# The four factors of the update of q in PSUM instead of SBUF

## The chip, the cores and the metric

One core of one Trainium2 chip runs the kernel. The metric is the device time of one execution in microseconds (us); lower is better. Engines are named as in the profile: PE is TensorE (PEld its weight loads), DVE is VectorE, ACT is ScalarE, POOL is GpSimd, SP is SyncE.

## The reference

The input x holds 16 sequences of 128 steps with 256 features. It drives an oscillator network, one Runge-Kutta step of fourth order per time step, and every q of it then goes through a feed-forward layer of eight experts (the best two taken) and a shared expert. The result is added to x.

```
def _derivative(q, p, drive, coupling, bias):
    i_couple = jnp.tanh(q) @ coupling.T
    dq = q - q ** 3 / 3.0 - p + drive + i_couple + bias
    dp = EPSILON * (q + ALPHA - BETA * p)
    return (dq, dp)

def _rk4_step(q, p, drive, coupling, bias):
    dq1, dp1 = _derivative(q, p, ...)
    dq2, dp2 = _derivative(q + 0.5 * DT * dq1, p + 0.5 * DT * dp1, ...)
    dq3, dp3 = _derivative(q + 0.5 * DT * dq2, p + 0.5 * DT * dp2, ...)
    dq4, dp4 = _derivative(q + DT * dq3, p + DT * dp3, ...)
    q_next = q + DT / 6.0 * (dq1 + 2 * dq2 + 2 * dq3 + dq4)
    ...
    q_next = jnp.clip(q_next, -CLAMP, CLAMP)
...
logits = x @ W_router.T            # x is here the trace of q
combine = top 2 of softmax(logits)
sh = silu(x @ gate) * (x @ up) @ Ws_down, times sigmoid(x @ W_sgate.T)
eo = the same for each of 8 experts, weighed with combine
x_out = x_in + shared + sparse
```

The 128 steps depend on each other, and so do the four derivatives in a step: 512 stages that can only run one after the other.

## The kernel before

Features lie on the partitions: 256 features are 2 halves (KC) of 128 partitions, with 16 sequences (B) each, so that every tile of the recurrence is 128x32. The program is written out in full: BLOCKS = 16 blocks of STEPS = 8 steps, with STAGES = 32 stages in a block. The order on each engine is the order in which the code emits it, and semaphores connect the engines.

A stage n goes as follows. PE (`couple`) first adds the drive into the bank `coup_ps` by three matmuls of an identity (line 554), behind which stand, in some stages, up to six matmuls that write columns 256 to 383 of that bank and whose result nobody reads (L558, counts in `WARM`). It then waits for ACT's first tanh, `th_hi` in fp16 (L439), and multiplies it with the two fp16 parts of the coupling (L565, eight matmuls). Then it waits for `th_lo` (L820, DVE), the rest of the tanh, which DVE takes from ACT's second tanh in PSUM (`th`, L440), and multiplies it (L571, four matmuls). The last of these counts up `summands`. DVE meanwhile works out the cubic term (L813 or ACT's L446, L817 or L824), the sums for p (L784), and `force` (L831), and then forms the next q:

```
dve.wait_ge(summands, 2 * (n + 1))
nc.vector.scalar_tensor_tensor(
    q_raw[:] if k == 3 else q_in[k + 1][:], coup_ps[:, 0:CB]...,
    c_un[:, ...], force[:], ALU.mult, ALU.add).then_inc(q_ready, 1)
```

This is line 848, once in each of the 512 stages. It multiplies the coupling with a factor and adds `force`. The factor is one value for each partition: a column of `c_un`, worked out on the chip before the first stage (L718: `unscale`, a power of two that depends on the coupling's largest element, times the step's constant C[k]). The instruction gets it as the address of a 128x1 operand, a pointer scalar. L784, L813, L817, L824 and L831 are the same kind of instruction (scalar_tensor_tensor) with their factor written in the instruction as a constant. `q_ready` releases ACT's tanh (L439), DVE's own square (L813) or clip (L794), and PE's next drive matmuls (L554).

Behind `couple` of each stage PE takes pieces of the feed-forward layer of the block before and of the one before that: router (L584), `comb` turned and spread (L592, L603), up projections (L629), down projections (L646). Tables such as `UP_AT` and `DOWN_AT` say in which stage. ACT and DVE have their parts of it (L480, L488; L895, and `route`, L859 to L873) between the recurrence's instructions.

Before the first stage DVE prepares the scales and constants one after the other; each `step` counts up `setup_v`. Step 10 is `ident_u` (L716), step 11 is `c_un` (L718), step 12 is `p_now` (L721).

Of the kernel before, what the change touches and what calls it, by code (L numbers as in the profile page):

```python
# [28 lines left out]
P = 128  # L29
# [130 lines left out]
def program(nc, x, cond, coupling, bias, w_up, w_down, w_route, identity, spread, iota, e_base, out):  # L160
    ctx = ExitStack()
    with ctx:
        def sb(name, shape, dt=F32):
            return ctx.enter_context(nc.sbuf_tensor(name, shape, dt))

        def pb(name):
            return ctx.enter_context(nc.psum_tensor(name, [P, 512], F32))

        def sem(name):
            return ctx.enter_context(nc.semaphore(name))  # L170
# [27 lines left out]
        ebits = sb("ebits", [P, 2], U32)  # L198
        scale = sb("scale", [P, 2])
        unscale = sb("unscale", [P, 2])  # L200
        c_un = sb("c_un", [P, 4])

        q_trace = sb("q_trace", [P, KC, STEPS, B])
        q_raw = sb("q_raw", [P, KC, B])
# [38 lines left out]
        coup_ps = pb("coup_ps")  # L243
# [4 lines left out]
        square_ps = pb("square_ps")  # L248
        th, square_first, square, cubic = [ps[:, c:c + CB].rearrange("p (m b) -> p m b", m=KC) for ps, c in (
            (th_ps, 0), (square_ps, 0), (square_ps, 2 * CB), (square_ps, 4 * CB))]  # L250
        comb_tp = route_ps[0:96, 64:128].bitcast(BF16)

        in_cf = sem("in_cf")
# [5 lines left out]
        setup_v = sem("setup_v")  # L259
# [100 lines left out]
        def upper(x, steps):  # L360

            return x[:, steps].rearrange("p t m b -> p (t m b)").bitcast(BF16)[:, 1::2]

        def flat(x, steps):

            return x[:, steps].rearrange("p t m b -> p (t m b)")
# [137 lines left out]
        def _(pe):  # L504
# [37 lines left out]
            def couple(b, st):  # L542

                n = b * STAGES + st
                if n == 0:
                    pe.wait_ge(setup_v, 10)
                else:
                    pe.wait_ge(q_ready, n)
                if st % (4 * HALF) == 0:
                    pe.wait_ge(x_split, 4 * b + 2 + 2 * (st // (4 * HALF)))  # L550
                t = b * STEPS + st // 4
                at = slice(t, t + 1)
                for x, piece in enumerate((upper(xb, at), upper(x_rest, at), flat(x_low, at))):
                    nc.tensor.matmul(coup_ps[:, 0:CB], ident_u[:], piece, start=x == 0, stop=False,  # L554
                                     skip_group_check=True)
                if n > STAGES:
                    for _ in range(WARM[st - 1]):
                        nc.tensor.matmul(coup_ps[:, 2 * P:3 * P], c16[:, 0, 0, 0:P], c16[:, 0, 0, 0:P],  # L558
                                         start=False, stop=True, skip_group_check=True)

                pe.wait_ge(hi_ready, n + 1)
                for part in range(2):
                    for m in range(KC):
                        for k in range(KC):
                            nc.tensor.matmul(coup_ps[:, m * B:(m + 1) * B], c16[:, part, k, m * P:(m + 1) * P],  # L565
                                             th_hi[:, k, :], start=False, stop=False, skip_group_check=True)

                pe.wait_ge(lo_ready, b * STAGES + st + 1)
                for m in range(KC):
                    for k in range(KC):  # L570
                        last = nc.tensor.matmul(coup_ps[:, m * B:(m + 1) * B], c16[:, 0, k, m * P:(m + 1) * P],  # L571
                                                th_lo[:, k, :], start=False, stop=True, skip_group_check=True)
                last.then_inc(summands, 1)
# [78 lines left out]
            def one_block(b):  # L652
                for st in range(STAGES):
                    couple(b, st)
                    prepare(b * STAGES + st)
                    if b == 1 and st == 0:
                        pe.wait_ge(in_wd, 2 * 16)
                        pe.wait_ge(in_const, 4 * 16)
                    for f, at in ffn_stages(b, st)[::-1]:
                        ffn(f, at)  # L660
                    if b == 0 and STAGES // 2 <= st < min(REST_AT):

                        for _ in range(8):
                            nc.tensor.matmul(up_ps[0][:, 0:P], c16[:, 0, 0, 0:P], c16[:, 0, 0, 0:P], start=True,
                                             stop=True)
# [358 lines left out]
```

## Time and profile before

| | |
|---|---|
| median of 3 runs | 655.67 us (655.66 to 658.51) |
| the profiled execution | 658.68 us |
| its span, first to last instruction | 656.9 us |
| granted TensorE clock, mean | 0.992 of full speed |
| busy share of the span | PE 97%, PEld 93%, DVE 93%, ACT 56%, POOL 30% |

Durations in the profile overlap where an engine is pipelined: an instruction on DVE can start while the records of the one ahead of it still run. So a busy share of 97% does not mean that the engine has no room. Distances from start to start, and from the end of one to the start of the one that waited for it, tell more.

### The profile page before, as it was taken

Reading aid. Unit: us, or ns where it says so; the run is one execution under the profiler, and the core shown is the slowest. Engines: PE = TensorE matmul, PEld = TensorE weight load, DVE = VectorE, ACT = ScalarE, POOL = GpSimd, SP = SyncE. Lnnn points to the kernel's source line nnn. Section 1 sums busy time; section 2 is a strip of 40 time slices with the busy share of each in tenths; the row PEclk is TensorE's granted clock in tenths of the full one; section 3 lists DMA queues with packets and bytes.
Section 4 is the critical chain, followed back from the end, with each engine's and each line's share of the span. In section 5 each row is a group of like instructions: output and inputs, shape, how many; then the busy total and the mean of one; then the engine's idle time right before and its main releaser. Section 6 shows DMA issues by size and latency. Waiting matters only on the chain.

```text
span 656.9 us, 33948 instructions
## 1 busy us (share of the span) xinstructions
PE 637.9 (97%) x12839; PEld 610.6 (93%) x12839; DVE 614.0 (93%) x4540; ACT 365.4 (56%) x1880; POOL 194.0 (30%) x436
## 2 busy tenths in 40 slices
PE   3899999999999999999999999999999999999998
PEld 2689899999999999999999999999999999999997
DVE  6998999999999999999999999999999999999951
ACT  4776655555555555556555555555556555554643
POOL 0002133242323334232333423233342323323244
PEclk9997999999999999999999999999999999999999
DMA  7800000000000000000000000000000000000000
GB/s 297 279 2 2 4 2 4 11 3 11 4 11 3 3 12 2 12 2 12 3 4 10 4 12 3 11 4 2 12 4 11 3 12 2 4 12 3 11 3 17
DMA packets 9059, 13.65 MB, mean 21 GB/s; under 512 B 1568, under 2 KB 8032, under 8 KB 8256
## 3 DMA queue, kind: packets, MB, share of 16 engines
q1 hardware_dynamic: 8896, 11.50, 5.2%
q8 instruction: 100, 1.64, 1.0%
q14 instruction: 63, 0.52, 0.3%
HBM read 9.40 MB, written 2.10 MB: 17 GB/s over the span
## 4 chain that ended last, share of the span: by engine, by line
PE 90%; DVE 8%; DMA 0%; issue 0%; ACT 0%; POOL 0%; DVEq 0%; SPq 0%
PE up_ps L629 28%; PE down_ps L646 21%; PE coup_ps L565 15%; PE coup_ps L571 13%; PE coup_ps L554 5%; PE coup_ps L558 3%; PE route_ps L603 2%; DVE q L848 1%; PE route_ps L584 1%; DVE w L772 1%; DVE force L831 1%; DVE th_lo L820 1%; DVE square_ps L817 1%; DVE square_ps L813 1%; DVE p_sum L784 1%; DVE y L784 0%
## 5 line engine op out<-in xcount | busy, mean ns | idle before, releaser
L629 PE MATMUL up_ps<-q_hi,w 128*128 128x128 f16 x2176 | 236.4, 219 | 0.2 <-POOL q_lo L926 0.2
L963 POOL TENSOR_TENSOR hidden<-hidden,comb_s 128x128 f32<-128x128 f32 x272 | 123.3, 456 | 297.7 <-ACT th_hi L439 290.2
L439 ACT ACTIVATE th_hi<-q 128x32 f16<-128x32 f32 x384 | 88.1, 229 | 213.6 <-DVE q L848 211.9
L629 PE MATMUL up_ps<-q_lo,w 128*128 128x128 f16 x1088 | 199.7, 220 | 0.0
L565 PE MATMUL coup_ps<-th_hi,c 128*128 128x16 f16 x4096 | 180.7, 171 | 0.2
L646 PE MATMUL down_ps<-hidden,wd 128*128 128x128 f32 x1088 | 180.8, 290 | 0.0
L629 PEld LDWEIGHTS up_ps<-q_hi,w 128*128 128x128 f16 x2176 | 176.2, 98 | 0.7 <-POOL q_lo L926 0.4
L565 PEld LDWEIGHTS coup_ps<-th_hi,c 128*128 128x128 f16 x4096 | 138.8, 96 | 4.6
L646 PEld LDWEIGHTS down_ps<-hidden,wd 128*128 128x128 f32 x1088 | 141.9, 191 | 0.0
L571 PE MATMUL coup_ps<-th_lo,c 128*128 128x16 f16 x2048 | 131.4, 173 | 0.4 <-DVE th_lo L820 0.3
L480 ACT ACTIVATE act_s<-up_ps,unscale 128x128 f32<-128x128 f32 x272 | 98.9, 364 | 13.8 <-PE up_ps L629 10.1
L629 PEld LDWEIGHTS up_ps<-q_lo,w 128*128 128x128 f16 x1088 | 105.9, 97 | 0.1
L554 PE MATMUL coup_ps<-xb,ident_u 128*128 128x32 bf16 x512 | 92.9, 181 | 10.1 <-DVE q L848 4.4
L571 PEld LDWEIGHTS coup_ps<-th_lo,c 128*128 128x128 f16 x2048 | 85.7, 97 | 16.2 <-DVE th_lo L820 0.7
L848 DVE SCALAR_TENSOR_TENSOR q<-coup_ps,c_un,force 128x32 f32<-128x32 f32 x384 | 96.3, 251 | 4.6 <-PE coup_ps L571 2.5
L820 DVE TENSOR_TENSOR th_lo<-th_ps,th_hi 128x32 f16<-128x32 f32 x512 | 97.8, 191 | 1.0 <-ACT th_ps L440 1.0
L554 PE MATMUL coup_ps<-x_rest,ident_u 128*128 128x32 bf16 x512 | 90.9, 178 | 0.0
L554 PE MATMUL coup_ps<-x_low,ident_u 128*128 128x32 bf16 x512 | 90.6, 177 | 0.0
L895 DVE TENSOR_TENSOR hidden<-act_s,up_ps 128x128 f32<-128x128 f32 x272 | 76.3, 281 | 13.2 <-ACT act_s L480 13.2
L813 DVE SCALAR_TENSOR_TENSOR square_ps<-q 128x32 f32<-128x32 f32 x384 | 76.6, 199 | 0.0
L817 DVE SCALAR_TENSOR_TENSOR square_ps<-square_ps,q 128x32 f32<-128x32 f32 x384 | 76.5, 199 | 0.0
L784 DVE SCALAR_TENSOR_TENSOR p_sum<-q,p_sum 128x32 f32<-128x32 f32 x384 | 71.0, 185 | 0.0
(107 smaller groups left out, 1098.8 us busy)
## 6 DMA issues: line engine op xcount, KB each, us to landing
wf<-in_w_up SPq DMA_DIRECT2D x4, 1056.0 KB, 8.3
wd<-in_w_down SPq DMA_DIRECT2D x1, 2048.0 KB, 21.0
out<-out_s SPq DMA_DIRECT2D x16, 128.0 KB, 2.2
xs<-in_x SPq DMA_DIRECT2D x1, 1920.0 KB, 17.3
sel<-in_spread SPq DMA_DIRECT2D x1, 408.0 KB, 17.1
cf<-in_coupling SPq DMA_DIRECT2D x1, 256.0 KB, 2.6
xs<-in_x SPq DMA_DIRECT2D x1, 128.0 KB, 2.4
ident<-in_identity SPq DMA_DIRECT2D x1, 64.0 KB, 2.5
```

The costliest lines, as they stand in the source:

```text
L439: nc.scalar.activation(th_hi[:], q[:], ACT.Tanh).then_inc(hi_ready, 1)
L480: nc.scalar.activation(act_s[:, j % 4, :], up_ps[(f * TILES + j) % UPS][:, 0:TOK], ACT.Silu, scale=unscale[:, 1:2]).then_inc(silu_ready, 1)
L554: nc.tensor.matmul(coup_ps[:, 0:CB], ident_u[:], piece, start=x == 0, stop=False, skip_group_check=True)
L565: nc.tensor.matmul(coup_ps[:, m * B:(m + 1) * B], c16[:, part, k, m * P:(m + 1) * P], th_hi[:, k, :], start=False, stop=False, skip_group_ ...
L571: last = nc.tensor.matmul(coup_ps[:, m * B:(m + 1) * B], c16[:, 0, k, m * P:(m + 1) * P], th_lo[:, k, :], start=False, stop=True, skip_gro ...
L629: last = nc.tensor.matmul(up_ps[(f * TILES + j) % UPS][:, h * TOK:(h + 1) * TOK], w16[:, part, k, h, j * P:(j + 1) * P], q[:, k, :], start ...
L646: last = nc.tensor.matmul(down_ps[:, m * TOK:(m + 1) * TOK], wd[:, j, m * P:(m + 1) * P], hidden[:, j, :], start=j == m == 0, stop=j == TI ...
L813: nc.vector.scalar_tensor_tensor(square, q, THIRD[k], q, ALU.mult, ALU.mult).then_inc(squared, 1)
L817: nc.vector.scalar_tensor_tensor(cubic, square, LINEAR[k], q, ALU.subtract, ALU.mult).then_inc(cubed, 1)
L820: nc.vector.tensor_tensor(th_lo[:], th, th_hi[:], ALU.subtract).then_inc(lo_ready, 1)
L848: nc.vector.scalar_tensor_tensor(q_raw[:] if k == 3 else q_in[k + 1][:], coup_ps[:, 0:CB].rearrange("p (m b) -> p m b", m=KC), c_un[:, (0, ...
L963: nc.gpsimd.tensor_tensor(hidden[:, j, :], hidden[:, j, :], comb_s[:, j, :], ALU.mult).then_inc(weighed, 1)
```

## The change

`c_un` is no tile in SBUF any more. It is a name for four unused columns, 384 to 387, of the PSUM bank `coup_ps`, the same bank whose first 32 columns L848 reads. L718 writes them there and L848 takes its pointer scalar from there. Since PE writes this bank too, PE's first stage now waits for step 11 of the set-up and not for step 10. Nothing else changes: each engine has the same instructions in the same order.

```
@@ -198,7 +198,6 @@
         unscale = sb("unscale", [P, 2])
-        c_un = sb("c_un", [P, 4])
@@ -248,6 +247,7 @@
             (th_ps, 0), (square_ps, 0), (square_ps, 2 * CB), (square_ps, 4 * CB))]
+        c_un = coup_ps[:, 3 * P:3 * P + 4]
         comb_tp = route_ps[0:96, 64:128].bitcast(BF16)
@@ -543,7 +543,7 @@
                 if n == 0:
-                    pe.wait_ge(setup_v, 10)
+                    pe.wait_ge(setup_v, 11)
                 else:
                     pe.wait_ge(q_ready, n)
```

## Rows read from the trace of the kernel before

**Rows 1.** The page: busy time by engine, and the chain that ended last.
```profile
PE 637.9 (97%) x12839; PEld 610.6 (93%) x12839; DVE 614.0 (93%) x4540; ACT 365.4 (56%) x1880; POOL 194.0 (30%) x436
PE 90%; DVE 8%; DMA 0%; issue 0%; ACT 0%; POOL 0%; DVEq 0%; SPq 0%
```

**Rows 2.** Timeline of one stage (start us, duration us, engine, line).
```profile
301.46 0.25 DVE L848 SCALAR_TENSOR_TENSOR q<-coup_ps,c_un,force 128x32 f32<-128x32 f32 x1
301.63 0.18 DVE L784 SCALAR_TENSOR_TENSOR rest<-q,y 128x32 f32<-128x32 f32 x1
301.75 0.23 ACT L439 ACTIVATE th_hi<-q 128x32 f16<-128x32 f32 x1 [0.44 <-DVE q L848]
...
301.88 0.18 ACT L440 ACTIVATE th_ps<-q 128x32 f32<-128x32 f32 x1
...
302.10 0.19 DVE L820 TENSOR_TENSOR th_lo<-th_ps,th_hi 128x32 f16<-128x32 f32 x1
...
302.34 0.26 PE L571 MATMUL coup_ps<-th_lo,c 128*128 128x16 f16 x4
...
302.64 0.25 DVE L848 SCALAR_TENSOR_TENSOR q<-coup_ps,c_un,force 128x32 f32<-128x32 f32 x1
```

**Rows 3.** Line 848: durations, first and last start, who waited for it.
```profile
L848 DVE SCALAR_TENSOR_TENSOR q<-coup_ps,c_un,force x384: 239/251/253, 10.7 to 627.6; 128x32 f32<-128x32 f32 x192
L848 DVE SCALAR_TENSOR_TENSOR q_raw<-coup_ps,c_un,force x128: 244/251/253, 14.4 to 628.8; 128x32 f32<-128x32 f32 x128
...
  ACT th_hi L439: 259.8, 489
```

**Rows 4.** Timeline of a stage with much feed-forward work on PE.
```profile
298.50 0.19 DVE L820 TENSOR_TENSOR th_lo<-th_ps,th_hi 128x32 f16<-128x32 f32 x1
...
298.79 0.24 PE L571 MATMUL coup_ps<-th_lo,c 128*128 128x16 f16 x4
```

**Rows 5.** Groups: the same kind of DVE instruction with and without pointer scalar (busy us, mean ns).
```profile
L831 DVE SCALAR_TENSOR_TENSOR force<-rest,square_ps 128x32 f32<-128x32 f32 x256 | 47.7, 186 | 0.0
L772 DVE SCALAR_TENSOR_TENSOR w<-wf,scale,w 128x128 f16<-128x128 f32 x28 | 9.6, 345 | 0.0
L772 DVE SCALAR_TENSOR_TENSOR w<-wf,scale,w 128x256 f16<-128x256 f32 x3 | 1.4, 478 | 0.0
L730 DVE SCALAR_TENSOR_TENSOR x_rest<-xb 128x128 f32<-128x128 f32 x32 | 9.1, 284 | 0.0
```

**Rows 6.** Groups: DVE instructions that read SBUF, PSUM or both, or write PSUM.
```profile
L784 DVE SCALAR_TENSOR_TENSOR rest<-q,y 128x32 f32<-128x32 f32 x256 | 47.1, 184 | 0.0
L895 DVE TENSOR_TENSOR hidden<-act_s,up_ps 128x128 f32<-128x128 f32 x272 | 76.3, 281 | 13.2 <-ACT act_s L480 13.2
L747 DVE TENSOR_REDUCE most<-w_sum 128x1 f32<-128x12 f32 x1 | 0.2, 156 | 0.0
L750 DVE TENSOR_REDUCE most<-route_ps 1x1 f32<-1x128 f32 x1 | 0.3, 272 | 0.0
L861 DVE TENSOR_REDUCE top<-logit 128x1 f32<-128x8 f32 x16 | 2.5, 154 | 0.0
L859 DVE COPY logit<-route_ps 128x9 f32<-128x9 f32 x16 | 2.6, 162 | 0.7 <-PE route_ps L584 0.7
L813 DVE SCALAR_TENSOR_TENSOR square_ps<-q 128x32 f32<-128x32 f32 x384 | 76.6, 199 | 0.0
```

**Rows 7.** Groups: ACT instructions that read SBUF or PSUM.
```profile
L488 ACT COPY comb_s<-route_ps 128x128 f32<-128x128 f32 x272 | 59.1, 261 | 1.5 <-PE route_ps L603 1.4
L411 ACT ACTIVATE ident_neg<-ident 128x128 f16<-128x128 f32 x1 | 0.3, 293 | 0.0
```

**Rows 8.** Timeline of the set-up's end.
```profile
8.79 0.28 DVE L718 TENSOR_SCALAR c_un<-unscale 128x1 f32<-128x1 f32 x3
...
9.65 0.29 DVE L734 SCALAR_TENSOR_TENSOR x_low<-x_rest 128x128 bf16<-128x128 f32 x1
...
10.09 0.18 PE L554 MATMUL coup_ps<-xb,ident_u 128*128 128x32 bf16 x1 [3.97 <-DVE x_low L734]
```

More of the change, by code:

```diff
@@ L200, in program @@
         unscale = sb("unscale", [P, 2])
-        c_un = sb("c_un", [P, 4])
         q_trace = sb("q_trace", [P, KC, STEPS, B])
@@ L250, in program @@
             (th_ps, 0), (square_ps, 0), (square_ps, 2 * CB), (square_ps, 4 * CB))]
+        c_un = coup_ps[:, 3 * P:3 * P + 4]
         comb_tp = route_ps[0:96, 64:128].bitcast(BF16)
@@ L545, in couple @@
                 if n == 0:
-                    pe.wait_ge(setup_v, 10)
+                    pe.wait_ge(setup_v, 11)
                 else:
```

## Prediction

> **What bounds the kernel now.** I read the page first. PE is busy for 97% of the span, and the chain that ended last runs through PE for 90% of it [rows 1]. This looks like a kernel that PE alone bounds, in which a slower or faster instruction on DVE would be hidden. But those records overlap, so the question is whether PE waits, and the timeline of one stage answers it. From one L848 to the next it goes: L848 takes 0.25 and ends at 301.71; L439 starts at 301.75, that is 0.04 later, when the semaphore has come through; the two tanh run from 301.75 to 302.06; `th_lo` starts at 302.10 and ends at 302.29; the matmuls on it start at 302.34 and end at 302.60; the next L848 starts at 302.64 [rows 2]. Each link starts 0.04 to 0.05 behind the end of the one ahead of it, which is as short as such a hand-over gets here, and the links make up the whole 1.18 us. So the recurrence's latency, and L848 with it, sets the stage. PE fills its waits so well that they don't show as idle time. The view of line 848 agrees: ACT's first tanh waited for it 489 times, 259.8 us in total [rows 3].
>
> Not every stage is of this kind. Where PE has more feed-forward work, it comes late: at 298.50 `th_lo` starts, it ends at 298.69, and the matmuls start at 298.79 [rows 4]. That is 0.10 instead of 0.05. In the steady part I find this in 7 of a block's 32 stages (numbers 10, 11, 19, 24, 25, 28 and 29), with some 25 ns of lateness in each; there PE would take up an added delay of up to 25 ns and give back nothing of a shortened one.
>
> The first L848 starts at 10.7 us and the last at 628.8 us [rows 3], with 511 stages between them. By the share above, 25/32 of them, 399 stages, pass a change of L848's duration on in full, and 112 do not (a gain) or only beyond 25 ns (a loss). The 28 us behind the last L848 are the last feed-forward layer, and the 10.7 us in front are loads and set-up. So the whole forecast is one sum: **399 times the change of L848's duration, in ns**. The instruction also holds up those behind it on DVE, but these (L784 at 301.63, and then the square, which waits for `q_ready` as ACT does) lie behind the same event and shift with it; they add no term of their own.
>
> **The change part by part.**
>
> *The set-up.* PE's first stage waits for step 11 (L718) instead of step 10. The three L718 run from 8.79 to 9.07, and PE's first L554 starts at 10.09, released by L734, which ended at 9.94 [rows 8]. So the new wait is over 0.87 us before the old one, and costs nothing. If L734 were not there, it would cost the 0.28 us of L718, once. That L718 now writes PSUM can cost some 15 ns each (L813, which writes PSUM, takes 199, and L784, which writes SBUF, 184 [rows 6]), also once, 0.05 us in all.
>
> *The pointer scalar from SBUF, removed.* L848 takes 251 ns [rows 3]. L831 reads one tile of PSUM and one of SBUF as well, has the same size and writes SBUF, but its factor is a constant: 186 ns [rows 5]. So the pointer scalar costs 65 ns. A second pair says the same: L772 with a pointer scalar takes 345 and L730 with a constant 284, both 128 elements, 61 ns more [rows 5]. It is a price that stands by itself in front of the streaming and is not hidden by it.
>
> *The pointer scalar from PSUM, added.* No row of this trace has it, so I bound it. It is a read, and the rows tell whether a read of PSUM takes DVE longer than one of SBUF. L831 (one input in PSUM) against L784 (both in SBUF): 186 and 184, +2 ns. L895 (PSUM and SBUF) against L730: 281 and 284, -3. These two could hide a short PSUM read behind the SBUF one, so rows that read PSUM alone matter more. An element costs (478 - 345)/128 = 1.04 ns [rows 5]. L750 reduces 128 elements from PSUM in 272 ns and L747 12 elements from SBUF in 156: 116 elements more are worth 121 ns, so 277 would be even, and PSUM is 5 ns shorter. L859 copies 9 elements from PSUM in 162; L861 reads 8 from SBUF in 154, so PSUM is 7 ns longer, though the operation is another [rows 6]. **So the difference between the two reads lies between -5 and +7 ns.** If a pointer read follows tensor reads, L848 goes from 251 to between 246 and 258. I take +2 ns, the value of the pair that is nearest in size and kind (L831 and L784), which is 0.8 us.
>
> The outer bounds are further off. Below, no more can be saved than the price of the pointer read, 65 ns, so 399 x 65 = 25.9 us. This is an upper limit, since PE would be late in more stages by then. Above, the nearest row that would double the price is the pointer read itself: if PSUM took one more access of that length, +65 ns.
>
> *Contention.* L848 reads the bank that PE writes, before as now. It is released by the last matmul of the stage, and PE's next write there (L554, and L558 behind it) waits for `q_ready`. So no second engine is in this bank while the factor is read. PE writes other banks all the time, but it did so while L831 and L895 read PSUM, and they aren't slower than their SBUF pairs.
>
> **The sum.** 658.68 us is the profiled execution (span 656.9, and 1.8 around it). 658.68 + 0.8 + 0.05 is 659.5. Against the median of the runs shown, 655.67, which is 3.0 below the profiled one, it is 656.5. The forecast is for such a median: **656.5 us**. What a measurement of this kernel can tell from no change is about 0.5%, 3.3 us, or 8 ns in each of the 399 stages.
>
> **The rivals.**
>
> *The same price (my forecast).* -5 to +7 ns: 399 x -5 = -2.0 and 399 x 7 = +2.8, so 653.7 to 658.5, all within 0.5%. For it speak four comparisons, none of which shows more; against it, that all are of tensors streamed, and none of a pointer scalar. Chance 0.45.
>
> *The pointer comes faster from PSUM.* The pointer read may have a path of its own, and the price of 65 ns may be SBUF's. ACT shows that the memory can matter: L488 reads 128 elements from PSUM in 261, L411 as many from SBUF in 293, 32 ns less [rows 7]. If DVE's pointer read saves as much, it is 399 x 32 = 12.8 us, so 643. If it costs nothing at all, 25.9 us, 630. Against it speak L750 and L859, which read PSUM alone on DVE and gain nothing like it. It decides from 8 ns saved. Chance 0.27, most of it between 640 and 652.
>
> *The pointer comes slower from PSUM, a little.* A pointer scalar and a tile in the same memory may have to take turns on one path, where before the pointer came from SBUF and the tile from PSUM. The price could be that of a PSUM write, 15 ns: 399 x 15 = 6.0, and 112 x 0 since PE's lateness covers it, 662. At 40 ns it is 399 x 40 + 112 x 15 = 17.6 us, 673. Against it: L772 has its pointer and its tiles all in SBUF, and pays 61, not more than L848's 65. Chance 0.14.
>
> *The pointer read doubles.* The price of the pointer is one access to the memory that it lies in, and DVE's access to PSUM is twice as long as to SBUF. That would be +65 ns: 399 x 65 + 112 x 40 = 25.9 + 4.5 = 30.4 us, so 686. For it speaks only that the 65 ns look like one whole access. Against it speaks that no row shows a longer access to PSUM: by it L859 should take some 60 ns more than L861 and takes 8 more. Chance 0.14. The Trainium skill, "Perfetto Trace Analysis", section "Optimizing Scalar/DVE Operations", states this rule: a data-access overhead of about 60 ns for DVE on SBUF and about 125 ns on PSUM. By its figures the sum would be +65 ns as well, an estimate of 686 us. The first figure agrees with the 61 to 65 ns of the pointer [rows 5], the second is not seen in any tile that DVE reads from PSUM here [rows 6].
>
> **How the numbers follow.** Faster by over 0.5% is the second case, 0.27. Within 0.5% is the first, 0.45. Slower by over 0.5% is the third and the fourth, 0.28. The first alone would give 653.7 to 658.5. To hold 8 in 10 the range takes in the slower case up to 40 ns (near 672) and the faster one to a little beyond ACT's 32 ns (640). Left out are the doubled access (0.14) and the faster case's far end (some 0.06).
>
> **What would show it right or wrong.** L848's mean is the one number that decides: 246 to 258 for my forecast, some 219 for ACT's saving, some 316 for the doubled access. The stage's period should move by exactly as much where the links are tight, and the lateness in stages like that of 298.79 should grow if L848 gets shorter and vanish if it gets longer by over 25 ns. L831, L784, L820 and the tanh should keep their durations; if one of them moves, something else than the pointer read is at work. PE's first L554 should still start near 10.09 and be released by L734. The forecast fails if a pointer read does not behave as a read of a tile does.

## The result, and the profile after

The changed kernel takes 660.47 us (median of 9 runs, 657.78 to 660.94), the kernel before 656.88 (median of 9, 655.66 to 658.53). The ratio is 1.0034 with a 95% interval of 1.0019 to 1.0049: slower by 0.34%, within the 0.5% that I took for no change. The two medians themselves are 3.6 us (0.55%) apart; they say less than the ratio, since the runs of each kernel fall into groups some 2 to 3 us apart (last section). The forecast of 656.5 us was for a median like that of the first three runs, 655.67; the median of nine is 1.2 us above that already. The profiled executions, 658.68 us before and 660.94 after, differ by 2.26 us, and their spans by 2.2 us.

Line 848 in the changed kernel, from the view of that line (minimum, median, maximum in ns; first and last start in us); it answers to [rows 3]:

```profile
L848 DVE SCALAR_TENSOR_TENSOR q<-coup_ps,force x384: 243/255/257, 10.6 to 629.8; 128x32 f32<-128x32 f32 x192
L848 DVE SCALAR_TENSOR_TENSOR q_raw<-coup_ps,force x128: 247/255/257, 14.3 to 631.0; 128x32 f32<-128x32 f32 x128
```

251 ns have become 255 (means: 250.7 and 255.0). The first and the last start tell where the time went: the set-up ends at the same time (10.6 and 10.7), and the last L848 is 2.2 us later (631.0 and 628.8), which is the whole difference of the spans.

Groups of the changed kernel, for [rows 5] and [rows 6]:

```profile
L848 DVE SCALAR_TENSOR_TENSOR q<-coup_ps,force 128x32 f32<-128x32 f32 x384 | 97.9, 255 | 4.7 <-PE coup_ps L571 2.5
L831 DVE SCALAR_TENSOR_TENSOR force<-rest,square_ps 128x32 f32<-128x32 f32 x256 | 47.8, 187 | 0.0
L784 DVE SCALAR_TENSOR_TENSOR rest<-q,y 128x32 f32<-128x32 f32 x256 | 47.0, 184 | 0.0
L718 DVE TENSOR_SCALAR coup_ps<-unscale 128x1 f32<-128x1 f32 x3 | 0.3, 155 | 0.0
```

Of the groups of more than 8 instructions on DVE and ACT, only those of L848 have means that moved by over 2 ns; L831 and L784 are where they were, to 1 ns. L718 takes 155 ns instead of 147, three times.

One stage of the changed kernel on the timeline, for [rows 2]:

```profile
301.50 0.26 DVE L848 SCALAR_TENSOR_TENSOR q<-coup_ps,force 128x32 f32<-128x32 f32 x1
...
301.79 0.23 ACT L439 ACTIVATE th_hi<-q 128x32 f16<-128x32 f32 x1 [0.39 <-DVE q L848]
...
302.14 0.19 DVE L820 TENSOR_TENSOR th_lo<-th_ps,th_hi 128x32 f16<-128x32 f32 x1
...
302.38 0.26 PE L571 MATMUL coup_ps<-th_lo,c 128*128 128x16 f16 x4
...
302.68 0.26 DVE L848 SCALAR_TENSOR_TENSOR q<-coup_ps,force 128x32 f32<-128x32 f32 x1
```

The links hand over as before, each 0.03 to 0.05 after the end of the one ahead, and only the first one is longer. From one L848 to the next both timelines read 1.18 us, since 4 ns are below their last digit, so I took the starts of all 512 L848 in both traces. From the 97th on, the distance from one to the next is 4.3 ns longer on average in 25 of a block's 32 stages, and 0.6 ns longer in the other seven, which are the seven that the prediction names as late. In those, PE's matmuls start 95 to 98 ns behind the end of `th_lo` instead of 101 to 103: PE's lateness took up the 4 ns.

### The profile page after: what moved, and what is told of

Its sections match the earlier page's. It is cut to its first block, busy times and chain, and to the rows that moved or that the text cites. A ratio compares the mean times of both kernels' runs of the same rounds, so it can differ in the third digit from the quotient of the medians.

```text
span 659.1 us, 33948 instructions
## 1 busy us (share of the span) xinstructions
PE 640.2 (97%) x12839; PEld 611.7 (93%) x12839; DVE 616.0 (93%) x4540; ACT 365.4 (55%) x1880; POOL 194.8 (30%) x436
## 4 chain that ended last, share of the span: by engine, by line
PE 91%; DVE 8%; issue 0%; DMA 0%; ACT 0%; POOL 0%; DVEq 0%; SPq 0%
PE up_ps L629 27%; PE down_ps L646 21%; PE coup_ps L565 16%; PE coup_ps L571 13%; PE coup_ps L554 5%; PE coup_ps L558 3%; PE route_ps L603 2%; PE route_ps L584 1%; DVE q L848 1%; DVE w L772 1%; DVE th_lo L820 1%; DVE force L831 1%; PE up_ps L539 1%; DVE square_ps L817 1%; DVE square_ps L813 0%; DVE p_sum L784 0%
## 5 line engine op out<-in xcount | busy, mean ns | idle before, releaser
L554 PE MATMUL coup_ps<-xb,ident_u 128*128 128x32 bf16 x512 | 92.8, 181 | 10.2 <-DVE q L848 4.4
L848 DVE SCALAR_TENSOR_TENSOR q<-coup_ps,force 128x32 f32<-128x32 f32 x384 | 97.9, 255 | 4.7 <-PE coup_ps L571 2.5
L554 PE MATMUL coup_ps<-x_rest,ident_u 128*128 128x32 bf16 x512 | 90.8, 177 | 0.0
L554 PE MATMUL coup_ps<-x_low,ident_u 128*128 128x32 bf16 x512 | 90.5, 177 | 0.0
L784 DVE SCALAR_TENSOR_TENSOR p_sum<-q,p_sum 128x32 f32<-128x32 f32 x384 | 70.8, 184 | 0.0
```

Source lines behind the costliest of these rows:

```text
L848: nc.vector.scalar_tensor_tensor(q_raw[:] if k == 3 else q_in[k + 1][:], coup_ps[:, 0:CB].rearrange("p (m b) -> p m b", m=KC), c_un[:, (0, ...
```

## The experiments

Theory A: a pointer scalar costs DVE about 4 ns more when it lies in PSUM than when it lies in SBUF, whatever else the instruction reads, and the chain passes that on. The rivals each have a kernel that takes their cause away.

**Was it a moved tile?** Theory B: dropping `c_un` from SBUF moved the tiles behind it. The kernel is the changed one with an unused tile in the old place:

```
         unscale = sb("unscale", [P, 2])
+        c_pad = sb("c_pad", [P, 4])
```

> The changed kernel with an unused tile of the old size kept in SBUF where c_un lay, so that every other tile of SBUF has its old address. Theory A (a pointer scalar read from PSUM costs DVE 4 ns more than one from SBUF): nothing differs from the changed kernel, L848 takes 255 ns on average, and the ratio to the kernel before is 1.003 to 1.004. Theory B (the other SBUF tiles moved by 16 bytes and one of them reads slower in L848): L848 is back at 251 ns and the ratio is 1.000 within its interval.

Measured: ratio 1.0036 (1.0021 to 1.0052), 12 runs. Its line 849 is the old 848:

```profile
L849 DVE SCALAR_TENSOR_TENSOR q<-coup_ps,force 128x32 f32<-128x32 f32 x384 | 98.0, 255 | 5.0 <-PE coup_ps L572 2.9
```

255 ns with the old addresses. Theory B falls.

**Was it the shared bank?** Theory C: pointer and tile take turns in one bank. The kernel puts the factors into another bank, that of ACT's tanh, and lets L718 wait for the first tanh there:

```
-        c_un = coup_ps[:, 3 * P:3 * P + 4]
+        c_un = th_ps[:, 3 * P:3 * P + 4]
...
+            dve.wait_ge(tanh_ready, 1)
             for k in (0, 2, 3):
```

> c_un lies in PSUM, but in the bank th_ps and not in the bank whose first 32 columns L848 reads. Theory A (the 4 ns belong to any pointer read from PSUM): L848 takes 255 ns and the ratio is 1.003 to 1.004, as in the changed kernel. Theory C (the 4 ns come from the pointer and the tile lying in one bank and taking turns there): L848 takes 251 ns or less and the ratio is 1.000.

Measured: ratio 1.0052 (1.0035 to 1.0068), 10 runs.

```profile
L849 DVE SCALAR_TENSOR_TENSOR q<-coup_ps,th_ps,force 128x32 f32<-128x32 f32 x384 | 97.9, 255 | 4.3 <-PE coup_ps L571 2.0
```

255 ns in another bank too, so theory C falls. The ratio lies a little above what A expected. The intervals of this kernel and of the changed one overlap, and L848 is the same, so I read no difference into it: 8 of its 10 runs have a mean granted clock of 0.992 or less, against 10 of 27 of the kernel before beside it, and such runs are the longer ones (last section).

**Was it the new wait?** The kernel before with this part alone:

```
-                    pe.wait_ge(setup_v, 10)
+                    pe.wait_ge(setup_v, 11)
```

> The kernel before with one part of the change alone: PE's first stage waits for step 11 of the set-up and not for step 10; c_un stays in SBUF. By my prediction this wait is over 0.87 us before the one on L734, so the ratio is 1.000 within its interval and L848 stays at 251 ns. If the wait were what costs, the first L554 would start later than 10.09 us and the whole difference of 2 us would be here already.

Measured: ratio 0.9998 (0.9984 to 1.0012), 12 runs, L848 at 251 ns. The end of its set-up on the timeline, for [rows 8]:

```profile
8.67 0.28 DVE L718 TENSOR_SCALAR c_un<-unscale 128x1 f32<-128x1 f32 x3
...
9.53 0.29 DVE L734 SCALAR_TENSOR_TENSOR x_low<-x_rest 128x128 bf16<-128x128 f32 x1
...
9.96 0.19 PE L554 MATMUL coup_ps<-xb,ident_u 128*128 128x32 bf16 x1 [3.97 <-DVE x_low L734]
```

L554 is still released by L734. The wait is free, as worked out.

**Is it the memory, or a PSUM tile beside the pointer?** L848 reads a tile from PSUM in both kernels. Theory D is that only such an instruction pays. One kernel has two more pointers, on instructions that read their tiles from SBUF alone:

```
+        fac_s = sb("fac_s", [P, 1])
+        fac_p = square_ps[:, 3 * P:3 * P + 1]
...
+            nc.vector.memset(fac_s[:], P_IN_Y3)
+            nc.vector.memset(fac_p, P_IN_Y4)
...
-                    add(y3[:], p_now[:], P_IN_Y3, q0_of(i))
+                    add(y3[:], p_now[:], fac_s[:, 0:1], q0_of(i))
...
-                    add(y4[:], p_now[:], P_IN_Y4, q0_of(i))
+                    add(y4[:], p_now[:], fac_p, q0_of(i))
```

> The kernel before with two more pointer scalars: y3 (L784, both tiles in SBUF, 128 times) takes its factor from a column in SBUF, y4 (the same shape and kind, also 128 times) takes its factor from a column in PSUM, in the bank square_ps; L848 is left with its pointer in SBUF. With constants both take 182 ns. Theory A (a pointer from PSUM costs 4 ns more than one from SBUF, whatever the tiles): y3 takes 243 to 247 ns and y4 247 to 251. Theory D (the 4 ns arise only where the instruction reads a tile from PSUM too, on the same path): y3 and y4 take the same. The kernel as a whole is slower, y3 in front of the square by some 50 ns in 128 stages, 6.8 us, and y4 in front of L848 by up to 60 ns in some of its 128, so 7 to 14 us in all.

Measured: one run, 667.95 us, against a median of 658.27 for the kernel before on that chip, 9.7 more and within the 7 to 14, though a single run can be 2 to 3 us off. What decides here is the durations, 128 of each kind. Its groups, with the line of the kernel before that has both of the two instructions with constants:

```profile
L788 DVE SCALAR_TENSOR_TENSOR y<-p_now,square_ps,q_trace 128x32 f32<-128x32 f32 x128 | 31.8, 248 | 0.0
L788 DVE SCALAR_TENSOR_TENSOR y<-p_now,fac_s,q_trace 128x32 f32<-128x32 f32 x128 | 31.2, 244 | 0.0
L788 DVE SCALAR_TENSOR_TENSOR v<-p_now,q_trace 128x32 f32<-128x32 f32 x128 | 23.6, 184 | 0.0
...
L784 DVE SCALAR_TENSOR_TENSOR y<-p_now,q_trace 128x32 f32<-128x32 f32 x256 | 46.6, 182 | 0.2 <-issue 0.2
```

Same kind, size and tiles: 182 ns with a constant (`y3` and `y4` in the kernel before; `v`, a third such instruction, takes 184), 244 with a pointer in SBUF (`y3`), 248 with one in PSUM (`y4`). So the pointer costs 60 to 62 ns from SBUF and 64 to 66 from PSUM, with no PSUM tile beside it. This is the +4 of L848 again. Theory A stands, and D falls.

**How much of a change does the chain pass on, downwards?** The kernel before with no pointer in L848. It holds only for inputs with this coupling's scale:

```
-                    c_un[:, (0, 0, 2, 3)[k]:(0, 0, 2, 3)[k] + 1], force[:], ALU.mult, ALU.add
+                    C[(0, 0, 2, 3)[k]] * 2.0 ** -16, force[:], ALU.mult, ALU.add
```

> The kernel before with L848's factor written as a constant in the instruction (C[k] times 2^-16, the value that c_un holds for this input; for an input with another scale the constant would be wrong). It takes the pointer read away and leaves its place on the chain. By my prediction's sum L848 falls from 251 to about 186 ns and 399 of the 511 stages pass it on: 25.9 us less, a ratio near 0.961, as an upper limit, since PE becomes late in more stages. If PE has less room than that, the ratio is 0.97 to 0.985, and the lateness of L571 behind th_lo grows by the part that is not passed on. If the chain through L848 did not set the time at all, the ratio would be 1.000.

Measured: 634.13 us, ratio 0.9641 (0.9619 to 0.9663), and on a second occasion 634.21 us, ratio 0.9619 (0.9600 to 0.9638). Two stages of its timeline, the first with much feed-forward work on PE and the second without:

```profile
285.27 0.19 DVE L848 SCALAR_TENSOR_TENSOR q<-coup_ps,force 128x32 f32<-128x32 f32 x1
...
285.85 0.19 DVE L820 TENSOR_TENSOR th_lo<-th_ps,th_hi 128x32 f16<-128x32 f32 x1
...
286.20 0.24 PE L571 MATMUL coup_ps<-th_lo,c 128*128 128x16 f16 x4
...
286.48 0.19 DVE L848 SCALAR_TENSOR_TENSOR q<-coup_ps,force 128x32 f32<-128x32 f32 x1
...
291.09 0.19 DVE L848 SCALAR_TENSOR_TENSOR q<-coup_ps,force 128x32 f32<-128x32 f32 x1
...
291.67 0.19 DVE L820 TENSOR_TENSOR th_lo<-th_ps,th_hi 128x32 f16<-128x32 f32 x1
...
291.92 0.26 PE L571 MATMUL coup_ps<-th_lo,c 128*128 128x16 f16 x4
...
292.21 0.19 DVE L848 SCALAR_TENSOR_TENSOR q_raw<-coup_ps,force 128x32 f32<-128x32 f32 x1
```

The second stage lasts 1.12 us (291.09 to 292.21) instead of 1.18: the 60 ns are passed on, and its matmuls start 0.06 behind `th_lo`. The first lasts 1.21 us. `th_lo` ends at 286.04 and its matmuls start at 286.20, 0.16 later: PE was not ready, and the gain became lateness. Over all stages from the 97th on the same: in the seven late positions of a block the distance between two L848 changed by 0.1 ns on average, in the other 25 by -60 to -62 ns. L848's mean is 191 ns, so 60 ns less, and 399 x 60 = 23.9 us. Measured are 24.1 us (658.23 - 634.13). I had taken 65 ns and 25.9 us, and had expected less than that since PE would be late in more stages; the count of stages held, and it was the 65 that was 5 too many.

**And upwards?** The kernel before with a pointer in another link of the chain, `th_lo`: it is multiplied by 1.0 from a column `one_s` in SBUF. The kind of instruction changes with it, from tensor_tensor to scalar_tensor_tensor:

```
-                nc.vector.tensor_tensor(th_lo[:], th, th_hi[:], ALU.subtract).then_inc(lo_ready, 1)
+                nc.vector.scalar_tensor_tensor(th_lo[:], th, one_s[:, 0:1], th_hi[:], ALU.mult, ALU.subtract
+                                               ).then_inc(lo_ready, 1)
```

> The kernel before with one more pointer scalar on the chain: th_lo (L820) becomes a scalar_tensor_tensor, th times a 1.0 from a column in SBUF minus th_hi, in all 512 stages. It lengthens the link by about 61 ns. If the share of stages that pass a delay on is what I counted (399 in full, 112 beyond 25 ns), the time rises by 399 x 61 + 112 x 36 = 28.4 us, ratio 1.043. If PE's fill gives more cover than that, it is below 1.03.

Measured: 685.96 us, ratio 1.0446 (1.0411 to 1.0481), 27.7 us more.

```profile
L822 DVE SCALAR_TENSOR_TENSOR th_lo<-th_ps,one_s,th_hi 128x32 f16<-128x32 f32 x512 | 128.3, 251 | 1.1 <-ACT th_ps L441 1.0
```

`th_lo` took 191 and takes 251. 399 x 60 + 112 x 35 = 27.9 us, near the 27.7 us of the medians. But the stages don't follow that sum. The profiled pair is 26.5 us apart, and by the starts of L848 (L851 here) from the 97th on, the median stage is longer by 61 ns in 19 of a block's 32 positions and by 34 on average in the seven late ones, which is as expected, but by only 38 in the other six. Those six are first stages of a time step (k = 0). One of them in the kernel before, and the same one in this kernel:

```profile
366.66 0.19 DVE L820 TENSOR_TENSOR th_lo<-th_ps,th_hi 128x32 f16<-128x32 f32 x1
...
366.91 0.26 PE L571 MATMUL coup_ps<-th_lo,c 128*128 128x16 f16 x4
...
367.12 0.18 DVE L784 SCALAR_TENSOR_TENSOR v<-p_now,q_trace 128x32 f32<-128x32 f32 x1
...
367.23 0.25 DVE L848 SCALAR_TENSOR_TENSOR q<-coup_ps,c_un,force 128x32 f32<-128x32 f32 x1
...
381.82 0.25 DVE L822 SCALAR_TENSOR_TENSOR th_lo<-th_ps,one_s,th_hi 128x32 f16<-128x32 f32 x1
...
382.13 0.26 PE L572 MATMUL coup_ps<-th_lo,c 128*128 128x16 f16 x4
...
382.32 0.18 DVE L786 SCALAR_TENSOR_TENSOR v<-p_now,q_trace 128x32 f32<-128x32 f32 x1
...
382.43 0.25 DVE L851 SCALAR_TENSOR_TENSOR q<-coup_ps,c_un,force 128x32 f32<-128x32 f32 x1
```

In the kernel before L848 starts 0.06 us behind the end of the last matmul (367.17), where it is 0.04 in the stage of [rows 2]. DVE is not ready sooner: in such a stage it has the cubic term, `p_sum`, `force` and `v` still to do behind `th_lo`, and L848 follows `v` by 0.11 us in both kernels (in all 95 such stages by 0.12 in the median, in both). So there DVE's own work sets the stage, and it covers some 20 of the 60 ns. 19 x 61 + 6 x 38 + 7 x 34 ns for each of the 16 blocks is 26.0 us; two stages that came out 0.3 and 0.5 us longer make up much of the rest. That 27.9 met 27.7 is in part luck (the runs lie between 685.05 and 688.95). A delay in L848 itself meets no such cover, since both DVE's work and the tanh start from it: there the six stages changed by as much as the other 19, in the changed kernel and in the one with the constant.

**A version that beats both.** The pointer exists only because the coupling's scale is worked out on the chip. With a constant scale it goes, and most of the set-up with it:

```
+C_SCALE = 2.0 ** 10
...
+            step(nc.vector.tensor_scalar(c16[:, 0], cf[:], C_SCALE, None, ALU.mult))
+            step(nc.vector.scalar_tensor_tensor(c16[:, 1], cf[:], C_SCALE, c16[:, 0], ALU.mult, ALU.subtract))
+            step(nc.vector.tensor_scalar(ident_u[:], ident[:], C_SCALE, None, ALU.mult))
...
+                    C[(0, 0, 2, 3)[k]] / C_SCALE, force[:], ALU.mult, ALU.add
```

> No pointer scalar in L848, and no scale worked out on the chip for the coupling: both fp16 parts and the identity are scaled by a constant 2^10, L848's factor is the constant C[k] times 2^-10, and the reductions, matmuls and power-of-two steps of the set-up for the coupling are gone (a coupling with elements up to 64 still fits fp16; a wider one would not, which the kernel before could take). L848 as in the kernel with the constant alone, 191 ns, so its 0.964 as a start; the set-up before the first L848 gets shorter by the steps between 5 and 7 us, but ACT's copy of x, which ends at 7.5 us, is needed too, so 1 to 1.5 us of it at most: 632 to 633 us, ratio 0.961 to 0.963.

> The kernel with the constant factor and the set-up of before once more, for a comparison with the fixed scale on the same chip: 634.1 us and 0.964 as measured before, L848 191 ns.

Measured on one chip: 630.35 us, ratio 0.9563 (0.9539 to 0.9586) for the fixed scale, and 634.21 us, 0.9619, for the constant factor alone. The fixed scale's line 834 is the old 848:

```profile
L834 DVE SCALAR_TENSOR_TENSOR q<-coup_ps,force x384: 176/191/193, 8.8 to 601.9; 128x32 f32<-128x32 f32 x192
```

It starts at 8.8 us instead of 10.7: 1.9 us from the set-up, over the 1.5 I allowed, and the ratio lies below the 0.961 to 0.963 that I expected. ACT's copy of x (L394) ends at 7.30 us instead of 7.52, and DVE takes it up 0.11 us later (at 7.41) instead of 1.80 us later (at 9.32), since L713 to L721 no longer stand in front. With 24 us from L848 it is 26 of the 28 us by which the medians differ. The rest is scatter: the two runs of this kernel with a mean granted clock of 0.992 took 632.24 and 632.81 us, and the median of the six such runs of the kernel before is 658.34, 25.5 to 26.1 more. Its price is generality: a coupling with elements of 64 or more no longer fits fp16 (64 x 2^10 is 65536, and the largest number of fp16 is 65504).

## Why the prediction was right, and where it was off

**Where the result lies.** 660.47 us is inside the whole range (640 to 672), 4.0 us above the forecast of 656.5 and above the 653.7 to 658.5 of its own first case. Of these 4.0 us, 1.2 are the median taken as a start, 655.67 instead of 656.88; 0.8 are the price of the pointer beyond the +2 ns, below. The remaining 2 us are most likely scatter: the median of the changed kernel falls into its longer group of runs, that of the kernel before between its groups. As a ratio, the measurement is in the first case.

**PE's 97% hides waits, and the recurrence's latency sets the stage.** Right. A DVE instruction that got 60 ns shorter made the kernel 24.1 us shorter, and one 60 ns longer made it 27.7 us longer. One part was missed: in the first stage of a time step DVE's own work behind `th_lo` ends last, by some 20 ns. It doesn't matter for L848.

**399 of 511 stages pass a change of L848 on.** Right, and seen position by position: the seven late stages are the predicted ones, in the changed kernel (+0.6 ns against +4.3) and with the constant factor (-0.1 against -60 to -62). The kernel with the constant gave -24.1 us where the count gives -23.9. The +27.7 us of the pointer in `th_lo` do not bear it out as they stand, as said there.

**The new wait costs nothing.** Right, by the kernel that has it alone (0.9998).

**The price of a pointer read from SBUF.** 65 ns by L831, 61 by L772 and L730. The runs showed 60 to 62 in three instructions (L848 251 to 191, `th_lo` 191 to 251, `y3` 182 to 244). L831 was a pair with a difference of 5 ns of its own: with a constant too, L848 takes 191 and L831 186. L848 reads its PSUM tile as the first input and L831 as the second; whether that is the reason was not tried.

**The price from PSUM.** This is the term that was mis-sized: I took +2 ns within -5 to +7, and it is +4. In the sum that is 399 x 4 = 1.6 us instead of 0.8. The profiled pair shows 2.2 us. From the 65th to the last L848 the difference grows by 1.55 us in 447 stages, 3.5 ns each, where the count gives 399/511 x 4.3 = 3.4. At that rate the first 40 stages make 0.14 us, but by the 41st L848, at 63 us, the difference is 0.56. So the remaining 0.4 us arise early. By then the granted clock of the two executions has fallen at different times (0.94 and 0.69 over 45 to 48 us, 0.77 and 0.95 over 56 to 60), but a part stands already before 45 us, and that part is not explained.

**The rivals.** That the pointer comes faster from PSUM, as ACT's reads suggested, is out: it is slower in L848 and in `y4`. That a pointer and a tile in PSUM take turns is out by `y4`, which has no tile in PSUM and pays the same 4 ns; the other bank takes out turns within one bank. That the pointer read doubles is out: 64 to 66 ns and not 125. The Trainium skill, "Perfetto Trace Analysis", section "Optimizing Scalar/DVE Operations", gives a data-access overhead of an instruction of about 60 ns for DVE on SBUF and about 125 on PSUM. The runs agree with the first, if it is taken for the price of a pointer read (60 to 62 ns), and not with the second (64 to 66 ns), and the measurement decides.

**The chances.** The 0.27 for "faster" rested on a row of another engine against two rows of DVE itself. The rows of DVE were the better witnesses and deserved more of it. No row ahead of the result held a pointer in PSUM, so that it came out within the -5 to +7 ns of tile reads was a likely case and no more.

## What to carry to other kernels

A share of 97% busy on PE is not yet a bound: follow one period from end to start over all engines, and if the hand-overs are all as short as they get, each nanosecond on that chain counts once in every period in which no other path is the later one. Here a change of L848 counted in 25 of 32 stages, and a longer `th_lo` in full only in 19, so ask it for the link in question. A pointer scalar cost the small DVE instructions here 60 ns, a third on top; moving it to the other memory changed 4 ns of that, and writing the factor as a constant saved all of it. Before asking where an operand should lie, ask whether the instruction needs it.

## What the runs showed of the hardware

A pointer scalar adds 60 to 62 ns to a scalar_tensor_tensor of 128x32 on DVE when it lies in SBUF and 64 to 66 when it lies in PSUM, whether a tile of PSUM is read beside it (L848, `th_lo`) or not (`y3`, `y4`), and in each of the three banks tried (`coup_ps`, `th_ps`, `square_ps`). That is as small a difference as the tiles of [rows 6] show, -5 to +7 ns. Writing a 128x1 column to PSUM instead of SBUF costs 8 ns (155 and 147).

The scatter of this kernel's runs, 655.66 to 658.53 us before the change, has to do with the TensorE clock early on. Sorted by mean granted clock, the runs of the kernel before beside the first experiments have medians of 658.73 us at 0.992 (9 runs), 656.9 at 0.997 (8) and 655.8 at 1.000 (2). The window of 45 to 60 us after the start, in the kernel before:

```profile
45.00:60.00 15.00, 14.61 (x231) 14.01 (x230) 12.33 (x93) 9.46 (x37) 2.52 (x3) 0.66 0.01 3
```

and in the kernel with the wait alone, whose L848 is the same:

```profile
45.00:60.00 15.00, 14.50 (x263) 13.81 (x264) 13.76 (x106) 10.58 (x43) 2.52 (x3) 0.89 0.01 3
```

The third number from the end is the granted clock as a share of the full one: a mean of 0.66 against 0.89 over the same 15 us, part of it at 1.2 GHz and the rest at 2.4 (over 48 to 56 us the first kernel has 0.50, the second 0.79). In the 15 us ahead of that, PE was busy for 14.46 us in the first kernel, at a granted clock of 1.00. In the first kernel DVE has 93 instructions in the window, in the second 106. The spans are 656.9 and 655.1 us, and the starts of L848 put the whole difference there: between the 29th (45.1 us) and the 37th (57.8 us) the second kernel gains 1.77 us, and behind that nothing. So the length of this stretch is worth about as much as the whole change that was studied here. Only several runs of each kernel tell them apart, or runs with the same mean clock. What decides the length was not tried.
